# Row statistics of the first stage: joining, offsets and mean squares from VectorE to GpSimd

## The reference, cut to what matters

```python
def _layernorm(x, axis=-1, eps=1e-05):
    m = jnp.mean(x, axis=axis, keepdims=True)
    v = jnp.var(x, axis=axis, keepdims=True)
    return (x - m) / jnp.sqrt(v + eps)

# first stage, inside _L0_attn_ref
proj = jnp.einsum('btd,ed->bte', x, W_in)
gate, val = (proj[..., :D], proj[..., D:])
g = jax.nn.sigmoid(gate)
v = conv(val, conv_w) + conv_b            # 5 taps per feature
h = a * h + g * v                         # a scan over the tokens gives y
res = x + jnp.einsum('btd,ed->bte', y, W_out)
mu = jnp.mean(res, axis=-1, keepdims=True)
var = jnp.mean(jnp.square(res - mu), axis=-1, keepdims=True)
attn = (res - mu) * jax.lax.rsqrt(var + LN_EPS) * ln_w + ln_b
...
x = _layernorm(x + attn)
# and in the second stage
sn = slots * jax.lax.rsqrt(jnp.mean(slots * slots, axis=-1, keepdims=True) + eps) * w
```

## Time and profile before

| what | before |
|---|---|
| median of 3 runs | 557.29 us (555.04 to 557.83) |
| profiled execution, own time | 557.2 us |
| profiled execution, span of the trace | 555.4 us |
| mean granted TensorE clock | 0.972 |
| PE busy | 507.8 us (91%) |
| DVE busy | 438.9 us (79%) |
| ACT busy | 343.8 us (62%) |
| POOL busy | 250.5 us (45%) |

### The profile page before, as it was taken

One profiled execution on the slowest core, in us unless ns is written; L12 is line 12 of the kernel. 1 busy time (PEld: TensorE's weight loads), 2 busy tenths in 40 slices (PEclk: granted clock), 3 DMA queues, 4 the chain that ended last, 5 costly groups with the idle time before them and its releaser, 6 DMA issues.

```text
span 555.4 us, 7269 instructions
## 1 busy us (share of the span) xinstructions
PE 507.8 (91%) x2174; PEld 366.0 (66%) x2174; DVE 438.9 (79%) x794; ACT 343.8 (62%) x608; POOL 250.5 (45%) x217
## 2 busy tenths in 40 slices
PE   6999986978779999899999999999997999979992
PEld 2465552845557687488768867885885788767771
DVE  2899999997799477989967985897677567868783
ACT  3657539786598474667466656765663766557453
POOL 0133050400223256556935664574335156737776
PEclk9999999899898999999999999999997999989997
DMA  8960202210021032000000000002111136255752
GB/s 299 316 194 2 76 1 76 76 44 33 0 77 63 15 77 77 0 2 0 2 1 1 0 0 1 2 1 76 40 38 39 38 128 235 91 159 157 222 153 71
DMA packets 28101, 39.98 MB, mean 72 GB/s; under 512 B 7421, under 2 KB 19838, under 8 KB 27776
## 3 DMA queue, kind: packets, MB, share of 16 engines
q1 hardware_dynamic: 24656, 31.10, 18.0%
q0 software_dynamic: 3408, 8.43, 4.1%
HBM read 25.70 MB, written 16.83 MB: 77 GB/s over the span
## 4 chain that ended last, share of the span: by engine, by line
PE 51%; DVE 6%; issue 6%; POOL 4%; ACT 3%; DMA 1%; SPq 0%; POOLq 0%; ACTq 0%; DVEq 0%
PE psum L1452 35%; PE psum L1542 7%; PE psum L1255 3%; PE psum L1394 2%; PE psum L1513 2%; PE psum L1340 1%; POOL gru L1005 1%; DVE gru L1865 1%; POOL sorted_rows L1035 1%; DVE slots_full L1867 1%; POOL out L1043 1%; POOL slots_lo L1020 1%; PE psum L1352 1%; DVE gru L1845 1%; PE psum L1416 1%
## 5 line engine op out<-in xcount | busy, mean ns | idle before, releaser
L1452 PE MATMUL psum<-slots_hi,w_hh 128*128 128x512 f32 x560 | 181.5, 406 | 1.2 <-ACT gru L752 1.2
L1452 PEld LDWEIGHTS psum<-slots_hi,w_hh 128*128 128x128 f32 x560 | 104.5, 191 | 27.8 <-issue 4.2
L1005 POOL TENSOR_TENSOR gru<-slots_full,gru 128x512 f32<-128x512 f32 x43 | 65.7, 1529 | 111.8 <-ACT gru L758 111.8
L1452 PE MATMUL psum<-slots_lo,w_hh 128*128 128x512 f32 x280 | 112.0, 400 | 0.0
L1452 PE MATMUL psum<-at,v_ih_pair 128*128 128x512 f32 x288 | 91.4, 402 | 5.0 <-DVE at L1744 3.1
L758 ACT ACTIVATE gru<-gru,vec 128x512 f32<-128x512 f32 x48 | 34.7, 722 | 58.7 <-DVE gru L1845 58.6
L1452 PEld LDWEIGHTS psum<-at,v_ih_pair 128*128 128x128 f32 x288 | 53.7, 190 | 21.9 <-DVE at L1744 3.4
L1838 DVE SCALAR_TENSOR_TENSOR gru<-psum,vec,gru 128x512 f32<-128x512 f32 x48 | 35.9, 747 | 36.0 <-PE psum L1452 30.2
L1138 PE MATMUL psum<-early_hi,w_in 128*128 128x512 f32 x128 | 57.9, 611 | 5.3 <-DMA early_hi<-in_xT 5.2
L1452 PEld LDWEIGHTS psum<-slots_lo,w_hh 128*128 128x128 f32 x280 | 53.4, 191 | 12.9
L1865 DVE TENSOR_TENSOR gru<-gru 128x512 f32<-128x512 f32 x47 | 43.7, 929 | 7.2 <-POOL gru L1005 3.7
(11 more groups left out here) (249 smaller groups left out, 878.3 us busy)
## 6 DMA issues: line engine op xcount, KB each, us to landing
gathered<-sorted_rows SPq DMA_DIRECT2D x39, 129.0 KB, 2.5
x_scratch<-slots_full SPq DMA_DIRECT2D x8, 512.0 KB, 3.0
x_block<-x_scratch SPq DMA_DIRECT2D x8, 512.0 KB, 4.1
early_hi<-in_xT SPq DMA_DIRECT2D x3, 1024.0 KB, 5.4
x_tm<-in_x SPq DMA_DIRECT2D x4, 512.0 KB, 6.3
slots_full<-expert_plus SPq DMA_DIRECT2D x1, 2048.0 KB, 10.3
sorted_rows<-gru SPq DMA_DIRECT2D x1, 1032.0 KB, 11.7
early_hi<-in_xT SPq DMA_DIRECT2D x2, 512.0 KB, 4.6
```

The costliest lines, as they stand in the source:

```text
L1005: pool.tensor_tensor(DF(u), full[:, c, seq(k, h), blk(j)], X(u), ALU.subtract).then_inc(d_pool, 1)
L1452: last = pe.matmul(psum[:, bank, :], w, d, start=start and i == 0, stop=stop and i == len(pairs) - 1, skip_group_check=begun or late)
```

## The change

Semaphores `agg1` and `agg2` now count POOL's operations, six per sequence. `bn_aggr` is gone. Where a row's two halves have means m1, m2 and summed squares s1, s2, POOL works out m1 + m2 and s1 + s2 (`joint`), ((m1 - m2) * 8)^2 (`apart`) and their sum (`spread2`), which is 256 times the variance. ACT's ln takes a scale of 1/256 instead. `st6` is held twice, once for each of the two norms. The offsets and the mean squares are POOL's as well. All of POOL's new operations take eight tiles at once: 128x16 or 128x8 elements.

The two core parts of the diff, POOL's functions and order, and DVE's:

```diff
-                        act.wait_ge(agg1, NT * n1)
+                        act.wait_ge(agg1, 6 * n1)
                     if n2 > 0:
-                        act.wait_ge(agg2, NT * n2)
-                    act.activation(rss[:, lo:hi], mvs[:, lo:hi, :, 1], ACT.Ln, bias=epsc[:, 2:3]).then_inc(ln_act, 1)
+                        act.wait_ge(agg2, 6 * n2)
+                    act.activation(rss[:, lo:hi], spread2[:, lo:hi], ACT.Ln, bias=epsc[:, 2:3],
+                                   scale=1.0 / D).then_inc(ln_act, 1)
...
-                def add_bias(b):
-                    for q in range(H2):
+                def add_bias(b, lo=0, hi=H2):
+                    for q in range(lo, hi):
...
+                def gather_halves(n, done, b):
+
+                    even, odd = st6[:, n, :, 1:3], st6[:, n, :, 4:6]
+                    pool.tensor_tensor(joint[:, n], even, odd, ALU.add).then_inc(done, 1)
+                    pool.tensor_tensor(apart[:, n], even[:, :, 0], odd[:, :, 0], ALU.subtract).then_inc(done, 1)
+                    pool.wait_ge(done, 6 * b + 2)
+                    pool.tensor_scalar(apart[:, n], apart[:, n], 0.5 * D ** 0.5, None, ALU.mult).then_inc(done, 1)
+                    pool.wait_ge(done, 6 * b + 3)
+                    pool.tensor_tensor(apart[:, n], apart[:, n], apart[:, n], ALU.mult).then_inc(done, 1)
+                    pool.wait_ge(done, 6 * b + 4)
+                    pool.tensor_tensor(spread2[:, n], joint[:, n, :, 1], apart[:, n], ALU.add).then_inc(done, 1)
+                    pool.tensor_scalar(joint[:, n, :, 0], joint[:, n, :, 0], -0.5, None, ALU.mult).then_inc(done, 1)
+
+                def first_spread(b):
+                    pool.wait_ge(bn1, NT * (b + 1))
+                    gather_halves(0, agg1, b)
+
+                def second_spread(b):
+                    pool.wait_ge(bn2, NT * (b + 1))
+                    gather_halves(1, agg2, b)
+
+                def first_offsets(b):
+                    pool.wait_ge(ln_act, 2 * FIRST[b] + 2)
+                    pool.tensor_tensor(nms[:, 0], joint[:, 0, :, 0], rss[:, 0], ALU.mult).then_inc(off1, 1)
+
+                def second_offsets(b):
+                    pool.wait_ge(ln_act, 2 * SECOND[b] + 2)
+                    pool.tensor_tensor(nms[:, 1], joint[:, 1, :, 0], rss[:, 1], ALU.mult).then_inc(off2, 1)
+                    pool.tensor_tensor(rrs[:, b], spread2[:, 1], rss[:, 1], ALU.mult).then_inc(ms_step, 1)
+                    pool.wait_ge(ms_step, 2 * b + 1)
+                    pool.tensor_tensor(rrs[:, b], rrs[:, b], rss[:, 1], ALU.mult).then_inc(ms_step, 1)
...
-                add_bias(0)
+                add_bias(0, 0, H2 - 1)
+                first_spread(0)
+                first_offsets(0)
+                add_bias(0, H2 - 1, H2)
+                second_spread(0)
                 gate_product(2)
-                add_bias(1)
+                add_bias(1, 0, H2 - 1)
+                first_spread(1)
+                first_offsets(1)
+                second_offsets(0)
+                add_bias(1, H2 - 1, H2)
+                second_spread(1)
+                second_offsets(1)
                 gate_product(3)
-                add_bias(2)
-                add_bias(3)
+                add_bias(2, 0, H2 - 1)
+                first_spread(2)
+                first_offsets(2)
+                add_bias(2, H2 - 1, H2)
+                second_spread(2)
+                second_offsets(2)
+                add_bias(3, 0, H2 - 1)
+                first_spread(3)
+                first_offsets(3)
+                add_bias(3, H2 - 1, H2)
...
                 difference(0, 0)
+                second_spread(3)
+                second_offsets(3)
                 difference(0, 1)
...
-                        dve.bn_stats(st6[:, t, :], res[:, b % 2, t, :]).then_inc(bn1, 1)
-                    if q == H2 - 1:
-                        dve.wait_ge(bn1, NT * (b + 1))
-                        for t in range(NT):
-                            dve.bn_aggr(mvs[:, 0, t, :], st6[:, t, :]).then_inc(agg1, 1)
...
-                def offsets(w):
-
-                    lo, hi, n1, n2 = WINDOWS[w]
-                    dve.wait_ge(ln_act, 2 * w + 2)
-                    if n1 > 0:
-                        dve.scalar_tensor_tensor(out=nms[:, 0], in0=mvs[:, 0, :, 0], scalar=-1.0, in1=rss[:, 0],
-                                                 op0=ALU.mult, op1=ALU.mult).then_inc(off1, 1)
-                    if n2 > 0:
-                        b = n2 - 1
-                        dve.scalar_tensor_tensor(out=nms[:, 1], in0=mvs[:, 1, :, 0], scalar=-1.0, in1=rss[:, 1],
-                                                 op0=ALU.mult, op1=ALU.mult).then_inc(off2, 1)
-                        dve.tensor_tensor(rrs[:, b], mvs[:, 1, :, 1], rss[:, 1], ALU.mult).then_inc(ms_step, 1)
-                        dve.wait_ge(ms_step, 2 * b + 1)
-                        dve.tensor_tensor(rrs[:, b], rrs[:, b], rss[:, 1], ALU.mult).then_inc(ms_step, 1)
...
                 residual(0)
                 tap_step(1, 1, 0)
-                offsets(0)
                 for i in range(1, TAPS):
...
                 scan(2, 0)
                 scan(2, 1)
                 taps(3, 0)
-                offsets(2)
                 residual(2)
                 tap_step(3, 1, 0)
-                offsets(3)
                 for i in range(1, TAPS):
                     tap_step(3, 1, i)
...
```

More of the change, by code:

```diff
@@ L96, in decoder_layer @@
         ident = sb("ident", [P, P])
-        sb("mean_place", [P, 2 * P])
+        st6 = sb("st6", [P, 2, NT, 6])
+        joint = sb("joint", [P, 2, NT, 2])
+        apart = sb("apart", [P, 2, NT])
+        spread2 = sb("spread2", [P, 2, NT])
+        sb("mean_place", [P, 2 * P - 20 * NT])
         ones_h = sb("ones_halves", [P, P], F32R)
@@ L334, in decoder_layer @@
         gates = sb1("gates", [P, 2, C, T])
-        st6 = sb1("st6", [P, NT, 6])
-        mvs = sb1("mvs", [P, 2, NT, 2])
         rss = sb1("rss", [P, 2, NT])
@@ L579, in row_roots @@
                     act.wait_ge(ms_step, 2 * b + 2)
-                    act.activation(rrs[:, b], rrs[:, b], ACT.Ln, bias=epsc[:, 0:1]).then_inc(rr_act, 1)
+                    act.activation(rrs[:, b], rrs[:, b], ACT.Ln, bias=epsc[:, 0:1], scale=1.0 / D).then_inc(rr_act, 1)
                     act.wait_ge(rr_act, 2 * b + 1)
@@ L1701, in second @@
                         for t in range(j * TJ, (j + 1) * TJ):
-                            dve.bn_stats(st6[:, t, :], res[:, b % 2, t, :]).then_inc(bn2, 1)
-                    if hi == J:
-                        dve.wait_ge(bn2, NT * (b + 1))
-                        for t in range(NT):
-                            dve.bn_aggr(mvs[:, 1, t, :], st6[:, t, :]).then_inc(agg2, 1)
+                            dve.bn_stats(st6[:, 1, t, :], res[:, b % 2, t, :]).then_inc(bn2, 1)
                 def hidden_parts():
@@ L1771, in _ @@
                 tap_step(2, 1, 0)
-                offsets(1)
                 for i in range(1, TAPS):
@@ L1786, in _ @@
                 scan(3, 0)
-                offsets(4)
                 first_tops()
@@ L1792, in _ @@
                 first_product()
-                offsets(5)
                 first_attention(0)
@@ L2124, in _ @@
                 second(3, 1, 2)
-                offsets(6)
                 candidate(0, 1)
```

1 line of the change is left out of this document (added).

## The result

| what | before | after |
|---|---|---|
| median | 556.69 us (4 runs) | 572.58 us (4 runs, 571.44 to 574.29) |
| ratio to before | 1 | 1.029 (95% interval 1.025 to 1.0331) |
| span of the trace | 555.4 us | 571.5 us |
| mean granted TensorE clock | 0.972 | 0.958 |

The account below looks back on a forecast made before the run. Relay latency from the last `bn_stats` to the first normalised row was taken to delay PE's second stage one for one. Terms 0.9 + 3.1 - 0.7 + 1.55 + 2.35 + 1.2 = +8.4 on 557.2 gave 565.6 us, range 555.5 to 571.

Parts of the forecast that it names:

- The key row: DVE and POOL operations on SBUF operands take turns; a 128x1024 DVE operation keeps POOL out about 1.1 us.
- the middle between the bounds: POOL's chain beside the four taps: 4.0 us if one gap takes two steps, 5.45 otherwise; 4.7 taken.
- The rivals in which the steps hardly meet VectorE: POOL's small steps slip in without waiting for taps, chain 1.1 us: 555.2 or 553 us; chance 0.13.
- in which VectorE is slowed: Some 45 small steps beside DVE operations cost DVE 0.2 us per handover: +5 on top, 571 us; chance 0.08.
- the taps' stretch: Behind the last `bn_stats`: POOL steps start 1.3 us apart, four taps take 5.4 to 6 us.
- then three dependent steps (scale, square, sum) before ln may start: POOL's chain ahead of ln: sum, difference, then these three; five steps, about 1.1 us alone.
- 1, sequence 0: `second(0)` at 8.15 us instead of 6.96 (+1.2), joins -0.57, POOL's steps beside scans +0.25: `residual(1)` +0.9 late.
- 2, sequence 1's rows: Third bias holds the tap 0.25 us; rows 5.75 us after the statistics against 2.67: +3.1.
- 3, given back in sequence 2: PE no longer waits 0.73 us for a residual in sequence 2: -0.7.
- 4, sequence 2's rows: Rows 5.5 us after sequence 2's last `bn_stats` against 3.94: +1.55.
- 5, sequence 3's rows: Fewer turns, chain 3.0 us (bounds 1.1 and 3.6); rows at 4.9 us against 2.54: +2.35.
- 6, window 6: From sequence 3's second-norm joins to the root's ln: 2.95 us instead of 1.7, +1.2.

Follow-up runs that it names:

- the one-sequence variant: Sequence 0's first statistics on POOL, added to the kernel with only sequences 0 to 2's second statistics there: 559.93 us; with keys and values copied first, 558.42 us.

## Why the prediction was right or wrong

The direction was right, the size not: 572.58 us stands above the range of 555.5 to 571.0 us, and 16.2 us above before where the sum said 8.4. Two steps failed: what ln waits for, and what follows from a late `window(0)`. The terms of steps 2 and 4 to 6 were short, mostly by the first of these, and the clock was not in the sum.

**The key row held.** POOL steps of 8 columns beside taps took 1.15 to 1.27 us and gaps took two steps now and then, as one end of the bounds had it. So the middle between the bounds was a fair choice. The five steps ended 85.52 - 81.13 = 4.4 us after the last `bn_stats` at sequence 1, where 4.7 was taken. The Trainium skill ("SBUF — State Buffer", "Who interferes with whom") gave exclusion for the whole instruction, and the trace agrees in that POOL got in only as a tap ended. That a scan of VectorE holds a small step for 2.1 to 2.2 us is this case's own number. The rivals in which the steps hardly meet VectorE, or in which VectorE is slowed, fell with the same rows: 5.47 us for four taps. The 571 us of the second of these lie nearest to the measured time, which is an accident. Of the signs, the taps' stretch came as described and ACT's wait grew by 12.10 - 9.14 = 3.0 us, as forecast; PE's transposes started at 105.41 us and not near 101.

**The step that failed first: "then three dependent steps (scale, square, sum) before ln may start".** Ln waits for a count of six, and the sixth step sits behind the sum, at the cost of one more tap: 1.2 us at each of sequences 0 to 2, 0.2 at 3, 0.7 at window 6. The text itself quoted the wait for six. Counting five in its place gives back 6.0 us of 16.2 in one edit, of which 1.7 in the traces is the clock at the sixteen matmuls; 4.4 are left, against 4.6 us of sixth steps. With this step in the sum, rows at sequence 1 would have stood at 5.75 + 1.2 = 6.95 us, and they came at 6.47.

The other steps can be set beside what each stretch of the path added, from the starts in the table of the first section:

| step of the prediction | forecast | in the traces | alone, by ratios |
|---|---|---|---|
| 1, sequence 0 | +0.9 | +4.6 | 4.0 |
| 2, sequence 1's rows | +3.1 | +3.8 | 3.2 with step 3 |
| 3, given back in sequence 2 | -0.7 | -3.2 | |
| 4, sequence 2's rows | +1.55 | +2.8 | 2.2 |
| not forecast, up to sequence 3's statistics | 0 | +1.6 | |
| 5, sequence 3's rows | +2.35 | +3.4 | 2.6 |
| 6, window 6 | +1.2 | +3.0 | 2.9 |
| sum | +8.4 | +16.0 | |

**Step 1** is the one that was furthest off. `second(0)` was put at 8.15 us after the last `bn_stats`; it came 53.95 - 43.59 = 10.4 us after it. Of this excess 1.2 is the sixth step and 1.1 are the copies of keys and values, which stand between exp and the rows. VectorE waited 4.17 us behind its taps, where 1 to 2.5 were forecast. Behind `second(0)` the forecast took 0.3 us off; in the trace 1.8 us came on instead (from 2.8 us late at `second(0)` to 4.6 at the last `bn_stats` of sequence 1), because `residual(1)` waited 1.81 us for PE, and PE had waited 4.32 us for the copies of keys. The step let VectorE alone set what follows; it did not list what else stands behind `window(0)` on ACT. Taking PE's wait away made sequence 1's statistics 4.0 us earlier in the trace, of which 2.3 were left at the root. The times show 1.6 us of it by ratios, uncertain by 3.2, and none on the one-sequence variant. What it is worth in the end stays open.

**Steps 2, 4 and 5** were short by 0.7, 1.3 and 1.0 us, about the sixth step each time (at sequence 3 it is rather the chain itself, 4.1 us to ln where 3.0 was taken: the pair of steps took 1.12 and 0.75 us beside DVE's product and cast). Taken alone on the chip sequences 2 and 3 came within 0.7 us of the forecast, and sequence 1 cost 3.2 where steps 2 and 3 together said 2.4.

**Step 3**: more came back than 0.7, because PE's transposes took 1.97 in place of 3.68 us, at a granted clock of 1.00 in place of 0.50. And 1.6 us went again at the sixteen matmuls of 5.35 us. **The clock was left out of the sum** in both directions: the granted clock of 48 to 71 us fell from 1.00 to 0.85, that of 97 to 130 us rose from 0.93 to 0.95. Its two largest effects on the path nearly cancel (-1.7 and +1.7).

**Step 6**: from the joins to the root it took 178.26 - 173.44 = 4.8 us where 2.95 was put. The chain of six ended after 2.1 us, of which 0.74 is the sixth, and the three products beside GRU mixes took 0.75, 0.20 and 1.07 us.

**The gain was under-counted.** The second statistics of sequences 0 to 2 were put at -0.3 (-0.57 + 0.25); the kernel with them alone measures -2.1. Their latency is hidden, as was said, and a bias of POOL no longer stands in the way of a tap (0.7 us of it). Had the forecast seen it, it would have been further off in the total: two errors of opposite sign.

## What to carry to other kernels

A chain of small dependent steps on GpSimd can cost not its work but its turns with the long operations of VectorE, up to one for each step: six steps that took 1.5 us alone took 5.4 beside them. So such work may go to GpSimd where nobody waits for it (here the second statistics, 2.1 us gained, a part of it by the place of a bias) and not where a relay of engines hangs on it, however idle GpSimd looks. And read each counted wait for what it includes: a step that the reader does not need, put last in the count, cost 4 to 6 of 16 us. And list for each engine of the relay what else stands behind the wait: here copies for another engine stood there, and a residual waited 1.81 us for what followed from them.

## What the runs showed of the hardware that was not expected

- POOL's steps of 128x8 and 128x16 took 0.20 to 0.23 us alone, 1.1 to 1.3 us beside VectorE's 128x1024 operations, 2.1 to 2.2 us beside its 128x1024 scan (2.3 us long). VectorE's own four taps hardly moved (5.47 against 5.42 us for four).
- Making VectorE wait for POOL ahead of its taps (2.18, 1.76 and 1.59 us at sequences 0 to 2) was 8.2 us faster than letting it run.
- Eight matmuls took 1.89 us without a wait ahead and 3.78 us after one of 4.32 us, at a granted clock of 1.00 and 0.50, which is 2.4 and 1.2 GHz. Sixteen others took 3.65 or 5.35 us (granted clock 1.00 and 0.68) with the same wait of 1.48 or 1.49 us directly ahead, from one kernel to another. Sixteen transposes took 3.68 us after a wait of 4.66 us, 1.97 after 3.14, and 3.45 after 2.46.
